# Cross attention on one core: another order of the three score banks within a step

## Chip, cores and metric

One NeuronCore of a Trainium2 chip runs the whole kernel. The metric is the device time of one execution in microseconds. All inputs and outputs are fp32.

## What is computed

The reference is one cross-attention layer with 32 heads of 32 columns, batch 2, 512 queries and 1024 keys per batch, hidden size 1024 (cut to what matters; `mu` and `var` are the mean and variance of a row):

```python
x = (hidden_states - mu) * rsqrt(var + 1e-5) * ln_gamma + ln_beta
Q = split_heads(x @ Wq.T);  K = split_heads(ctx);  V = split_heads(ctx)
scores = einsum('bhsd,bhtd->bhst', Q, K) * 32 ** -0.5
probs = softmax(where(mask, scores, -inf), axis=-1)
out = hidden_states + einsum('bhst,bhtd->bhsd', probs, V) @ Wout.T
```

## The kernel before

**Stages.** The kernel first normalises x and projects the queries (until about 141 us of the trace), then runs 16 attention steps (about 141 to 615 us), then multiplies the attention output by Wout and adds x (to the end). The change touches the attention steps alone.

**A step** is one batch and one group of four heads. Its 1024 keys are cut into eight tiles of 128; a tile with its four heads is a *slot*, `tt` = 0 to 7. So a step has 32 score blocks, numbered `at = 4 * tt + h`, 0 to 31. I call them score 0 to score 31, and their exponentials exp 0 to exp 31. For a score block:

- TensorE (L958, in `score`) multiplies a 99 x 128 block of keys with 99 x 512 of queries into one of three PSUM banks, `SX[at % 3]`.
- ScalarE (L624, in `exp`) reads that bank and writes the exponential into `PR`, a ring of four tiles in SBUF.
- TensorE (L974, in `values`) multiplies the four finished blocks of a tile with the values into the bank `PV`. This is called for the tile before the current one, so `values` of tile 7 runs within slot 0 of the next step.

**The wait that the change is about.** A score block may be written only after the exponential that last read its bank. Within a step, score `at` waits for exp `at - 3` (`pe.wait_ge(exp_done, PROBS * n + at - BANKS + 1)`, L953). For the first three scores of a step, L955 takes the last block of the step before that used the same bank. 32 blocks over three banks leave a remainder of two: score 30 uses bank 0 and score 31 uses bank 1, and the next step begins again with banks 0 and 1.

**What stands around it on TensorE.** The order is written out by hand in the table `STEP`. Per slot: scores 4tt and 4tt+1, the items `early`, `values` of the tile before, the items `with_01`, scores 4tt+2 and 4tt+3, the items `with_23`. The items are row maxima for the next steps (L934 on TensorE into one of two pairs of banks, `MX`, then a maximum on VectorE, L746), a transpose of keys (L874 in slot 0, copied by ScalarE at L550), a transpose of the maxima (L939), and the row sums of the step before (L964 in slot 1, 24 matrix multiplies with 32 columns of ones over the probabilities). All engines run their instructions in program order and wait on semaphores.

**The others.** GpSimd (L495) adds the probabilities of tiles 0 to 5 of a step into `acc`, five additions. ScalarE may overwrite a tile of `PR` only after GpSimd's addition that reads it. In slot 0, ScalarE also copies `PV` out (L628). SyncE issues the DMAs, among them the two bias rows (L350, L351) that score 0 of the next step waits for (`bias_in`).

**Where the steps stand in the program.** Step 0 is written out with a table of its own, `FIRST_STEP`. Steps 1 to 12 are three passes of a loop over four steps (`Fori`) on every engine. Steps 13, 14 and 15 are written out again. In step 15 the maxima are replaced by transposes of Wout (L944).

Of the kernel before, what the change touches and what calls it, by code (L numbers as in the profile page):

```python
# [27 lines left out]
ACT = mybir.ActivationFunctionType  # L28
# [4 lines left out]
P = 128  # L33
HPG = P // HD
# [7 lines left out]
RING = 4  # L42
MASK = 3 * HD
BIAS = MASK + 1
ROWS = BIAS + 2
SCALE = float(HD) ** -0.5
# [3 lines left out]
BIG = 1.75 * 2.0 ** 127  # L50
BANKS = 3
PROBS = TT * HPG
POOL_TILES = (0, 1, 2, 3, 4, 5)
DIRECT_TILES = (6, 7)
ADDS = len(POOL_TILES) - 1
DVE_T = 32
# [60 lines left out]
def is_first(n):  # L117

    return isinstance(n, int) and n == 0
# [57 lines left out]
def build(nc, x, ctx, mask, wq, wout, gamma, beta, out):  # L177
    def sb(name, shape, dt):
        return nc.alloc_sbuf_tensor(name, shape, dt)
# [11 lines left out]
    KS = [R[:, r * KSZ:(r + 1) * KSZ].rearrange("p (h t) -> p h t", h=HPG) for r in range(RING)]  # L191
    QS = [R[:, q_at[r]:q_at[r] + QSZ].rearrange("p (h s) -> p h s", h=HPG) for r in range(RING)]
# [22 lines left out]
    PR = sb("PR", [P, RING, HPG, S], F32)  # L215
# [32 lines left out]
    SX = [nc.alloc_psum_tensor(f"SX{i}", [P, S], F32) for i in range(BANKS)]  # L248
    PV = nc.alloc_psum_tensor("PV", [P, S], F32)
    QP = [PV, SX[2]]  # L250
# [19 lines left out]
    scores_ready, exp_done, tile_used, pool_used = sem("scores_ready"), sem("exp_done"), sem("tile_used"), sem("pool_used")  # L270
# [23 lines left out]
    with nc.Block() as block:  # L294
# [167 lines left out]
        def _(pool):  # L462
# [22 lines left out]
            def add_probs(n, k):  # L485

                first, tt = POOL_TILES[0], POOL_TILES[k + 1]
                if k == 0:
                    if not is_first(n):
                        pool.wait_ge(sums_done, n)  # L490
                else:
                    pool.wait_ge(pool_used, ADDS * n + ADDS + k)
                pool.wait_ge(exp_done, PROBS * n + HPG * (tt + 1))
                a = PR[:, first % RING, :, :] if k == 0 else acc[:, :, :]
# [25 lines left out]
        def _(act):  # L520
# [92 lines left out]
            def exp(n, tt, h):  # L613

                q = PROBS * n + HPG * tt + h
                if h == 0:

                    act.wait_ge(tile_used, TT * n + tt + 1)

                    old, m = (tt - RING, n) if tt >= RING else (tt + RING, n - 1)  # L620
                    if old in POOL_TILES:
                        act.wait_ge(pool_used, ADDS * m + ADDS + max(POOL_TILES.index(old), 1))
                act.wait_ge(scores_ready, q + 1)
                nc.scalar.activation(PR[:, tt % RING, h, :], SX[(HPG * tt + h) % BANKS][:, :], ACT.Exp, scale=SCALE).then_inc(exp_done, 1)  # L624

            def pv_copy(n):
                act.wait_ge(pv_done, n + 1)
# [16 lines left out]
            def step(n, items, at, first=False):  # L644
                for tt, (early, with_01, with_23) in enumerate(items):
                    exp(n, tt, 0)
                    exp(n, tt, 1)
                    if tt == 0 and not first:
                        pv_copy(n - 1)
                    at = high_and_bias(n, early + with_01, at)  # L650
                    exp(n, tt, 2)
                    exp(n, tt, 3)
                    at = high_and_bias(n, with_23, at)
                    if isinstance(n, int) and n == STEPS - 1 and tt == TT // 2:
                        first_attn_high()
# [206 lines left out]
        def _(pe):  # L862
# [84 lines left out]
            def score(n, u, tt, h):  # L947
                at = HPG * tt + h
                if at == 0:
                    pe.wait_ge(bias_in, 32 * (n + 1))  # L950

                if at >= BANKS:
                    pe.wait_ge(exp_done, PROBS * n + at - BANKS + 1)  # L953
                elif not is_first(n):
                    pe.wait_ge(exp_done, PROBS * n - PROBS + max(b for b in range(PROBS) if b % BANKS == at) + 1)  # L955
                elif SX[at] is QP[1]:
                    pe.wait_ge(q_copied, 2 + BATCH * GROUPS)
                nc.tensor.matmul(SX[at % BANKS][:, :], KS[u % RING][0:ROWS, h, tt * P:(tt + 1) * P], QS[u % RING][0:ROWS, h, :],  # L958
                                 start=True, stop=True).then_inc(scores_ready, 1)

            def sum_probs(bank, tile, start, stop):
# [6 lines left out]
            def values(n, u, tt):  # L968

                pe.wait_ge(exp_done, PROBS * n + HPG * (tt + 1))  # L970
                if tt == 0 and not is_first(n):
# [4 lines left out]
                if tt == TT - 1:  # L976
                    ins.then_inc(pv_done, 1)
                if tt in POOL_TILES:
                    ins.then_inc(tile_used, 1)
# [29 lines left out]
            at = 2 + len(WITH_GROUP[0])  # L1009
            pe.wait_ge(rows_in[0], FIRST_ROWS)  # L1010
            for g in range(1, GROUPS):
# [21 lines left out]
                at = end  # L1033
            pe.sem_inc(tile_used, RING)

            def step(n, u, items, at, loads, freed, first=False):
# [22 lines left out]
                for tt, (early, with_01, with_23) in enumerate(items):  # L1059
                    score(n, u, tt, 0)  # L1060
                    score(n, u, tt, 1)
                    for item in early:
                        mx_item(*item)
                    if tt >= 1:
                        values(n, u, tt - 1)
                    elif not first:
                        values(n - 1, u + RING - 1, TT - 1)
                    for item in with_01:
                        mx_item(*item)
                    score(n, u, tt, 2)  # L1070
                    score(n, u, tt, 3)
                    for item in with_23:
                        mx_item(*item)
# [3 lines left out]
            with pe.Fori(0, LOOPS) as j:  # L1077
                for u in range(1, RING + 1):
                    n = RING * j + u
# [3 lines left out]
            n = STEPS - 1  # L1083
# [49 lines left out]
```

## Time and profile before

| | |
|---|---|
| Median of 3 runs | 709.5 us (709.37 to 710.46) |
| The profiled execution | 710.47 us |
| Its span, first to last instruction | 708.6 us |
| TensorE busy, share of the span | 676.6 us, 95% |
| VectorE, ScalarE, GpSimd busy | 453.3, 339.4, 392.2 us |
| Mean granted TensorE clock | 0.998 |

The profile is of one execution. The 1.9 us between its time and its span lie before the first and after the last instruction. A busy TensorE is not a TensorE that issues at full rate: matrix multiplies overlap and their ends are modelled, so a late one shows as a longer one. The rows of its weight loads (PEld) carry the idle time and the releaser, and are read for waits.

### The profile page before, as it was taken

How to read it: one execution, taken by the hardware profiler on the slowest of the kernel's cores; microseconds unless marked ns; L12 is line 12 of the kernel's file. 1: busy time of each engine (PE TensorE's matmuls, PEld its weight loads, DVE VectorE, ACT ScalarE, POOL GpSimd, SP SyncE). 2: the span in 40 equal slices, each digit the busy share in tenths (PEclk: the TensorE clock that was granted, in tenths of full speed). 3: DMA queues.
4: the chain of work that ended last, by engine and by line, in shares of the span. 5: the costliest groups of instructions: out<-in, count | busy, mean ns of one | idle time of the engine just before them, and what ended most of it. 6: DMA issues, size and time to landing. Idle time of an engine off the chain costs nothing.

```text
span 708.6 us, 10761 instructions
## 1 busy us (share of the span) xinstructions
PE 676.6 (95%) x3537; PEld 395.6 (56%) x3537; DVE 453.3 (64%) x494; ACT 339.4 (48%) x614; POOL 392.2 (55%) x107
## 2 busy tenths in 40 slices
PE   2799999989999999999999999999999999999998
PEld 2577787844445454454544545445454454578886
DVE  6764343068878778687786877868778576633231
ACT  3641121256566665666656566565665666400000
POOL 1000000066679797697977979779797797900000
PEclk9999999999999999999999999999999999999999
DMA  9712000454624525245252452523515104033131
GB/s 337 196 39 71 31 30 1 93 123 108 149 59 108 128 64 138 56 110 122 67 138 65 100 125 65 138 65 100 134 32 134 61 7 144 31 118 114 65 118 59
DMA packets 40286, 68.10 MB, mean 96 GB/s; under 512 B 5668, under 2 KB 22694, under 8 KB 40238
## 3 DMA queue, kind: packets, MB, share of 16 engines
q1 hardware_dynamic: 39956, 67.25, 34.8%
q10 hardware_dynamic: 292, 0.40, 0.2%
q8 instruction: 17, 0.28, 0.2%
q14 instruction: 21, 0.17, 0.1%
HBM read 25.18 MB, written 4.19 MB: 41 GB/s over the span
## 4 chain that ended last, share of the span: by engine, by line
PE 89%; DVE 3%; ACT 3%; issue 2%; DMA 1%; SPq 1%; POOL 0%; ACTq 0%; DVEq 0%; POOLq 0%
PE MX L934 20%; PE PV L974 18%; PE SX L958 18%; PE MX L1092 12%; PE MX L964 5%; PE PV L897 5%; PE SX L897 5%; PE MX L874 2%; PE SX L889 1%; ACT PR L624 1%; PE MX L944 1%; DMA PR<-in_x 1%; ACT PR L534 1%; PE MX L868 1%; DVE R L705 1%
## 5 line engine op out<-in xcount | busy, mean ns | idle before, releaser
L746 DVE TENSOR_REDUCE mx<-MX 128x1 f32<-128x1024 f32 x256 | 301.8, 1216 | 87.3 <-PE MX L934 82.6
L624 ACT ACTIVATE PR<-SX 128x512 f32<-128x512 f32 x512 | 268.8, 600 | 161.2 <-PE SX L958 155.9
L495 POOL TENSOR_TENSOR acc<-acc,PR 128x2048 f32<-128x2048 f32 x64 | 293.7, 4589 | 8.7 <-POOL acc L495 5.4
L495 POOL TENSOR_TENSOR acc<-PR 128x2048 f32<-128x2048 f32 x16 | 73.5, 4594 | 219.1 <-ACT PR L624 219.1
L934 PE MATMUL MX<-R 97*128 97x512 f32 x512 | 174.5, 424 | 4.2 <-DMA R<-QT 1.5
L958 PE MATMUL SX<-R 99*128 99x512 f32 x512 | 174.0, 416 | 3.5 <-ACT PR L624 3.1
L934 PEld LDWEIGHTS MX<-R 97*128 97x128 f32 x512 | 84.5, 188 | 99.6 <-DVE mx L746 81.3
L974 PE MATMUL PV<-PR,C 128*32 128x512 f32 x1024 | 137.2, 608 | 0.1
L958 PEld LDWEIGHTS SX<-R 99*128 99x128 f32 x512 | 93.6, 189 | 66.5 <-ACT PR L624 35.5
L843 DVE TENSOR_TENSOR PR<-PR,MX 128x512 f32<-128x512 f32 x16 | 10.9, 686 | 53.3 <-PE MX L1092 51.7
L1092 PE MATMUL MX<-R 128*128 128x512 f32 x192 | 44.3, 390 | 0.0
L974 PEld LDWEIGHTS PV<-PR,C 128*32 128x32 f32 x1024 | 20.2, 108 | 41.2 <-ACT PR L624 36.4
L1092 PEld LDWEIGHTS MX<-R 128*128 128x128 f32 x192 | 36.0, 188 | 8.3 <-issue 0.8
L1092 PE MATMUL MX<-R,KTh 128*128 128x512 f32 x128 | 40.2, 390 | 0.0
L897 PE MATMUL PV<-R 128*128 128x512 f32 x120 | 32.3, 416 | 0.2 <-DVE R L705 0.2
L709 DVE TENSOR_TENSOR KTl<-MX,KTh 128x1024 fp32r<-128x1024 f32 x15 | 18.4, 1224 | 19.1 <-ACT KTh L550 19.1
L964 PE MATMUL MX<-PR,ones 128*32 128x512 f32 x240 | 28.5, 592 | 0.0
L1092 PEld LDWEIGHTS MX<-R,KTh 128*128 128x128 f32 x128 | 24.0, 188 | 5.8 <-issue 0.8
L483 POOL TENSOR_TENSOR QA<-QA,rsum 128x512 f32 (+1 forms) x16 | 20.6, 1289 | 11.4 <-DVE rsum L768 11.4
L572 ACT ACTIVATE QA<-SX 128x512 f32<-128x512 f32 x8 | 4.8, 599 | 44.3 <-PE SX L897 44.3
L897 PE MATMUL SX<-R,KTh 128*128 128x512 f32 x80 | 25.5, 389 | 0.0
L897 PEld LDWEIGHTS PV<-R 128*128 128x128 f32 x120 | 22.8, 199 | 4.8 <-DVE R L705 0.7
(84 smaller groups left out, 475.0 us busy)
## 6 DMA issues: line engine op xcount, KB each, us to landing
R<-KTh SPq DMA_DIRECT2D x60, 256.0 KB, 4.3
PR<-in_x SPq DMA_DIRECT2D x16, 512.0 KB, 4.1
C<-in_ctx SPq DMA_DIRECT2D x16, 512.0 KB, 3.4
R<-QT SPq DMA_DIRECT2D x62, 128.0 KB, 2.5
R<-KTl SPq DMA_DIRECT2D x60, 128.0 KB, 3.8
acc<-in_L_xattn_Wq SPq DMA_DIRECT2D x8, 512.0 KB, 3.7
C<-in_L_xattn_Wout SPq DMA_DIRECT2D x8, 512.0 KB, 3.4
R<-QT SPq DMA_DIRECT2D x62, 64.0 KB, 2.1
```

The source lines that it names most:

```text
L483: nc.gpsimd.tensor_tensor(at, at, rsum[:, :], ALU.mult).then_inc(attn_done, 1)
L495: nc.gpsimd.tensor_tensor(acc[:, :, :], a, PR[:, tt % RING, :, :], ALU.add).then_inc(pool_used, 1)
L624: nc.scalar.activation(PR[:, tt % RING, h, :], SX[(HPG * tt + h) % BANKS][:, :], ACT.Exp, scale=SCALE).then_inc(exp_done, 1)
L709: nc.vector.tensor_tensor(KTl[:, :], MX[par][:, :], KTh[:, :].bitcast(F32), ALU.subtract).then_inc(kt_lo, 1)
L746: nc.vector.tensor_reduce(mx[:, u % 2, i:i + 1], MX[par][:, :], mybir.AxisListType.X, ALU.max, negate=True).then_inc(mx_freed, 1)
L874: ins = nc.tensor.transpose(MX[par][:, t * P:(t + 1) * P], C[u % RING][:, t, :], ident[:, :])
L897: ins = nc.tensor.matmul(QP[b if bank is None else bank][:, :], w[W_IN[g]][:, k * P:(k + 1) * P], v[b][:, k, :], start=(k == 0 and o == 0) ...
L934: ins = nc.tensor.matmul(MX[par][:, cs], QS[u % RING][0:BIAS, h, st * P:(st + 1) * P], KS[u % RING][0:BIAS, h, cs], start=True, stop=True)
L958: nc.tensor.matmul(SX[at % BANKS][:, :], KS[u % RING][0:ROWS, h, tt * P:(tt + 1) * P], QS[u % RING][0:ROWS, h, :], start=True, stop=True). ...
L964: ins = nc.tensor.matmul(bank[h * HD:(h + 1) * HD, :], ones[:, :], tile(h), start=start, stop=stop, skip_group_check=True)
L974: ins = nc.tensor.matmul(PV[h * HD:(h + 1) * HD, :], C[u % RING][:, tt, h * HD:(h + 1) * HD], PR[:, tt % RING, h, :], start=(tt == 0), sto ...
L1092: ins = nc.tensor.matmul(MX[1 - q][:, cs], a[q][:, g, :], w[half][:, g, :], start=(g == 0 and o == 0), stop=(g == GROUPS - 1 and o == 2))
```

## The change

The bank of a score block is given by a new function `bank(b)`. Blocks 0 to 5 keep banks 0, 1, 2, 0, 1, 2. From block 6 on the order is turned by one: 6 uses bank 1, 7 bank 2, 8 bank 0, and so on, to 29 on bank 0, 30 on bank 1 and 31 on bank 2. The next step begins with bank 0 again. `before(b)` gives the block that used the bank of `b` last, as a negative number where it is in the step before: score 0 now waits for exp 29, score 1 for exp 30, score 2 for exp 31 of the step before. Score 6 now waits for exp 4 (before: exp 3), score 7 for exp 5 (before: exp 4), score 8 for exp 3 (before: exp 5). All others are as before.

```diff
+def bank(b):
+
+    return b % BANKS if b < HPG + 2 else (b + 1) % BANKS
+
+
+def before(b):
+
+    return max(c for c in range(-PROBS, b) if bank(c % PROBS) == bank(b))
...
-                nc.scalar.activation(PR[:, tt % RING, h, :], SX[(HPG * tt + h) % BANKS][:, :], ACT.Exp, scale=SCALE).then_inc(exp_done, 1)
+                nc.scalar.activation(PR[:, tt % RING, h, :], SX[bank(HPG * tt + h)][:, :], ACT.Exp, scale=SCALE).then_inc(exp_done, 1)
...
-                if at >= BANKS:
-                    pe.wait_ge(exp_done, PROBS * n + at - BANKS + 1)
-                elif not is_first(n):
-                    pe.wait_ge(exp_done, PROBS * n - PROBS + max(b for b in range(PROBS) if b % BANKS == at) + 1)
-                elif SX[at] is QP[1]:
+                if before(at) >= 0 or not is_first(n):
+                    pe.wait_ge(exp_done, PROBS * n + before(at) + 1)
+                elif SX[bank(at)] is QP[1]:
                     pe.wait_ge(q_copied, 2 + BATCH * GROUPS)
-                nc.tensor.matmul(SX[at % BANKS][:, :], KS[u % RING][0:ROWS, h, tt * P:(tt + 1) * P], QS[u % RING][0:ROWS, h, :],
+                nc.tensor.matmul(SX[bank(at)][:, :], KS[u % RING][0:ROWS, h, tt * P:(tt + 1) * P], QS[u % RING][0:ROWS, h, :],
                                  start=True, stop=True).then_inc(scores_ready, 1)
```

The order of work on TensorE stays; the banks, the values waited for and a few register instructions that compute these values move. Two places show it. First, TensorE where step 0 goes over into step 1: scores 30 and 31, the last maxima of the step, then scores 0 and 1 of the next and its `values`. Before:

```order
L958 MATMUL SX0<-R 128x512 [waits exp_done]
L958 MATMUL SX1<-R 128x512 [waits exp_done]
...
L1077 ISA
L955 ISA [waits bias_in]
L958 MATMUL SX0<-R 128x512 [waits exp_done]
L958 MATMUL SX1<-R 128x512 [waits exp_done]
L970 ISA
L974 MATMUL PV<-PR,C0 32x512 [waits exp_done]
```

And with the change:

```order
L968 MATMUL SX1<-R 128x512 [waits exp_done]
L968 MATMUL SX2<-R 128x512 [waits exp_done]
...
L1087 ISA
L965 ISA [waits bias_in]
L968 MATMUL SX0<-R 128x512 [waits exp_done]
L965 REGISTER_ALU
L968 MATMUL SX1<-R 128x512 [waits exp_done]
L980 ISA
L984 MATMUL PV<-PR,C0 32x512 [waits exp_done]
```

Bank 0 is now written three blocks before score 0, not two, and one register instruction stands between scores 0 and 1.

Second, TensorE in slot 1, after the row sums (the last of them reads `acc`): scores 6 and 7, one maximum, scores 8 and 9. Before:

```order
L964 MATMUL MX1<-acc,ones 32x512 x3
L958 MATMUL SX0<-R 128x512 [waits exp_done]
L953 REGISTER_ALU
L958 MATMUL SX1<-R 128x512 [waits exp_done]
L1042 REGISTER_ALU
L934 MATMUL MX0<-R 128x512 [waits mx_freed]
L934 MATMUL MX0<-R 128x512
L953 REGISTER_ALU
L958 MATMUL SX2<-R 128x512 [waits exp_done]
```

And with the change:

```order
L974 MATMUL MX1<-acc,ones 32x512 x3
L965 REGISTER_ALU
L968 MATMUL SX1<-R 128x512 [waits exp_done]
L965 REGISTER_ALU
L968 MATMUL SX2<-R 128x512 [waits exp_done]
L1052 REGISTER_ALU
L946 MATMUL MX0<-R 128x512 [waits mx_freed]
L946 MATMUL MX0<-R 128x512
L968 MATMUL SX0<-R 128x512 [waits exp_done]
```

Scores 6 and 7 now take the banks of scores 4 and 5, and a register instruction has moved from ahead of score 8 to ahead of score 6.

## Rows read from the trace of the kernel before

**Rows 1.** The page, busy time of each engine
```profile
PE 676.6 (95%) x3537; PEld 395.6 (56%) x3537; DVE 453.3 (64%) x494; ACT 339.4 (48%) x614; POOL 392.2 (55%) x107
```
**Rows 2.** Who waited for whom: us in total, times, longest us
```profile
PEld MX L934 <- DVE mx L746: 81.3, 121, 1.0
PEld PV L974 <- ACT PR L624: 36.4, 111, 0.4
PEld SX L958 <- ACT PR L624: 35.5, 123, 2.0
```
**Rows 3.** Busy time per engine from score 0 of step 6 to score 0 of step 7
```profile
320.22:349.54 29.32, 29.32 (x162) 14.18 (x161) 22.91 (x24) 18.52 (x36) 24.20 (x7) 1.00 0.40 99
```
**Rows 4.** Timeline, entry to step 6: start, duration, instruction, [idle before it <- releaser]
```profile
319.33 2.36 DVE L746 TENSOR_REDUCE mx<-MX 128x1 f32<-128x1024 f32 x2 [0.46 <-PE MX L934]
...
319.57 2.27 ACT L624 ACTIVATE PR<-SX 128x512 f32<-128x512 f32 x4 [1.08 <-PE SX L958]
319.57 4.59 POOL L495 TENSOR_TENSOR acc<-acc,PR 128x2048 f32<-128x2048 f32 x1 [0.16 <-POOL acc L495]
319.60 0.63 PE L934 MATMUL MX<-R 97*128 97x512 f32 x2
320.22 0.19 PEld L958 LDWEIGHTS SX<-R 99*128 99x128 f32 x1 [0.42 <-ACT PR L624]
...
320.70 0.19 PEld L958 LDWEIGHTS SX<-R 99*128 99x128 f32 x1 [0.30 <-ACT PR L624]
321.14 0.16 PEld L974 LDWEIGHTS PV<-PR,C 128*32 128x32 f32 x8 [0.25 <-issue]
...
322.13 0.30 PEld L934 LDWEIGHTS MX<-R 97*128 97x128 f32 x2 [0.84 <-DVE mx L746]
```
**Rows 5.** Timeline, the same pattern inside a step (step 5, slots 3 to 4)
```profile
306.25 2.07 ACT L624 ACTIVATE PR<-SX 128x512 f32<-128x512 f32 x4 [1.65 <-PE SX L958]
306.28 0.63 PE L934 MATMUL MX<-R 97*128 97x512 f32 x2
...
306.90 0.19 PEld L958 LDWEIGHTS SX<-R 99*128 99x128 f32 x1 [0.19 <-ACT PR L624]
...
307.38 0.16 PEld L974 LDWEIGHTS PV<-PR,C 128*32 128x32 f32 x8 [0.30 <-ACT PR L624]
```
**Rows 6.** Timeline, weight loads at the entries to step 2 and to step 14
```profile
202.59 0.19 PEld L958 LDWEIGHTS SX<-R 99*128 99x128 f32 x1 [0.30 <-ACT PR L624]
203.02 0.16 PEld L974 LDWEIGHTS PV<-PR,C 128*32 128x32 f32 x8 [0.25 <-issue]
...
555.76 0.19 PEld L958 LDWEIGHTS SX<-R 99*128 99x128 f32 x1 [0.24 <-ACT PR L624]
...
556.19 0.16 PEld L974 LDWEIGHTS PV<-PR,C 128*32 128x32 f32 x8 [0.25 <-issue]
```
**Rows 7.** Timeline, entry to step 1
```profile
172.92 0.42 PEld L958 LDWEIGHTS SX<-R 99*128 99x128 f32 x2
```
**Rows 8.** Timeline, entry to step 5, where the loop turns: exp 0, score 3
```profile
292.68 1.09 ACT L624 ACTIVATE PR<-SX 128x512 f32<-128x512 f32 x2 [2.19 <-issue]
...
293.33 0.19 PEld L958 LDWEIGHTS SX<-R 99*128 99x128 f32 x1 [0.83 <-ACT PR L624]
```
**Rows 9.** Timeline, entry to step 15: scores 0 and 1, values
```profile
584.24 0.52 PEld L958 LDWEIGHTS SX<-R 99*128 99x128 f32 x2
...
584.99 0.16 PEld L974 LDWEIGHTS PV<-PR,C 128*32 128x32 f32 x8 [0.24 <-issue]
```
**Rows 10.** Timeline, slot 1 of step 6: exps 4 and 5, scores 6 and 7
```profile
325.25 1.08 ACT L624 ACTIVATE PR<-SX 128x512 f32<-128x512 f32 x2
...
328.19 0.30 PEld L958 LDWEIGHTS SX<-R 99*128 99x128 f32 x2 [0.84 <-issue]
```
**Rows 11.** The last bias DMA before step 6, and such DMAs' us to landing
```profile
316.88 0.59 SPq L351 DMA_DIRECT2D R<-BTl  x1
...
R<-BTl SPq DMA_DIRECT2D x16, 8.0 KB, 1.8
```

## The prediction

> **What bounds the kernel now.** I read the page first. TensorE is busy 95% of the span, no other engine over 64% [rows 1], so what counts in the attention steps is what delays TensorE. The busy share hides this: over one step TensorE reads as busy for all 29.32 us, VectorE for 22.91, ScalarE for 18.52, GpSimd for 24.20 [rows 3], because a late matrix multiply is booked as a long one. The weight loads show the waits. Next I read who waited for whom: weight loads waited 35.5 us in total for exponentials ahead of scores, in 123 places, and 36.4 us ahead of values, in 111 [rows 2]. Most of this only mirrors the rate of the matrix multiplies. So the question has to be put place by place: when does a weight load start later than the instructions ahead of it on TensorE would let it?
>
> At the entry to a step it does. The last maximum of step 5 starts at 319.60 on TensorE. The load for score 0 comes at 320.22 after 0.42 us idle for an exponential, the one for score 1 at 320.70, after another 0.30, and the values of the last tile at 321.14 [rows 4]. ScalarE began exp 30 at 319.57 [rows 4]. Four exponentials in a row take 2.07 us where nothing holds them [rows 5], the last of them counted to its end at about 0.60, so they start (2.07 - 0.60) / 3 = 0.49 apart. Exp 30 then ends at 319.57 + 0.60 = 320.17 and exp 31 at 320.66. Score 0 started 0.05 after the end of exp 30 and score 1 about 0.05 after the end of exp 31: these are exactly the two waits that the remainder of two causes.
>
> The same stretch inside a step shows how it runs without them. There the maximum starts at 306.28, the second score at 306.90 and the values at 307.38, 1.10 us after the maximum [rows 5]. At the entry it takes 321.14 - 319.60 = 1.54 [rows 4]. The difference is 0.44 us.
>
> **What the change takes away.** Score 0 now waits for exp 29, which is over; score 1 for exp 30 (over at 320.17); and values, as before, for exp 31. So values can start at 320.66 + 0.05 = 320.71 and not at 321.14, a gain of 0.43. It can't be more, since values read what exp 31 writes. Both ways of working it agree, so I take 0.43 a place. Now the places, of the 15 entries:
>
> - *Entries to steps 2 to 4, 6 to 8 and 10 to 14, eleven in all.* They show the same pattern. From score 1 (just behind exp 31) to values it is 203.02 - 202.59 = 0.43 at the first and 556.19 - 555.76 = 0.43 at the last [rows 6]. 11 x 0.43 = 4.73 us.
> - *Entry to step 1.* Both loads run together without a wait [rows 7], since three maxima stand behind score 31 in that table. Zero.
> - *Entries to steps 5 and 9, where the loop turns.* ScalarE starts exp 0 only at 292.68 after 2.19 us that nothing explains but its own issue, and score 3, which needs exp 0's bank before and after, waits 0.83 for it [rows 8]. Values would come earlier, but the next score pair would not. Bounds: 0 and 0.43 each. I take 0, since that wait follows at once.
> - *Entry to step 15.* Scores 0 and 1 at 584.24 and values at 584.99 [rows 9]: 0.75, where the loads of a pair with no wait between them take 0.30 [rows 10]. Bounds 0 and 0.45. Half of it may be lost to ScalarE, which is the next to be waited for, so I take 0.2.
>
> Sum: 4.73 + 0.2 = 4.9 us.
>
> **What it adds, and what moves.**
>
> - *Scores 6 and 7 wait for exps 4 and 5.* These start at 325.25 and are over at 326.33; scores 6 and 7 are loaded from 328.19 on, behind the values and the 24 multiplies of the row sums [rows 10]. The cover is 328.19 - 326.33 = 1.86 us. Cost zero. Score 8 waits for an older exponential than before: nothing.
> - *A register instruction between scores 0 and 1* and one moved ahead of score 6. Scores 6 and 7 have one between them today and their two loads still take 0.30 us together [rows 10]. Score 1 has from 320.22 to 320.71 to be ready. Cost zero; from above, 0.1 at each of twelve places in the loop, 1.2 us.
> - *The bias rows.* Score 0 also waits for them. Issue at 316.88 and 1.8 us to landing [rows 11] give 318.7, while score 0 would now start about 0.4 earlier than 320.22, at 319.8. Still 1.1 us to spare.
> - *VectorE.* The first maximum after the values needs the `MX` half that the first of two reductions frees, 319.33 + 1.18 = 320.5 [rows 4]; it would start at 322.13 - 0.43 = 321.70. Free.
> - *GpSimd.* Its last addition ends at 319.57 + 4.59 = 324.16 [rows 4], and exp 4 may not start before, because it overwrites the tile. Exp 4 starts at 325.25 today [rows 10], at 324.82 with the change: 0.66 us are left. GpSimd's five additions begin with exp 7 of their step, so they move along and the rest does not shrink from step to step. This is the nearest thing that is late next.
>
> The profiled execution took 710.47 us, which gives 710.47 - 4.9 = 705.6. It is 1.0 above the median of 709.5, so for the median I forecast **704.6 us**.
>
> **Rivals.**
>
> 1. *The wait only moves.* Today the next bank is always the one free longest, except at the entry. The change puts the short distance in slot 1. If scores 6 and 7 stalled there for as long as 0 and 1 do today, the gain is given back, 15 x 0.43 against 11 x 0.43: about 709.5. Against it speaks the cover of 1.86 us. The Trainium skill ("Perfetto Trace Analysis", section on optimizing tensor performance, matmuls) says that independent groups should rotate through different PSUM banks so that the reading of one overlaps the next group; by this rule writing banks 1, 2, 1, 2 is worse than 1, 2, 0, 1, and this rival's time would be the result. The rows speak against it here, since the rule does not ask what stands between the two writes. 9%, together with the case that something I don't see binds every step.
> 2. *Half of it is swallowed downstream,* by GpSimd or by ScalarE, whose exp 4 has only 0.66 us left: 2.4 us gained, 707.1. For it: cover that thin at each step. Against: the distance is the same at each step. 8%.
> 3. *More.* Entries to 5 and 9 pay too, and step 15 in full: 13 x 0.43 + 0.45 = 6.0, so 703.5. 8%.
> 4. *Slower.* TensorE runs in order, so if exp 5 ended later than score 7 wants, row maxima and all behind it would wait. ScalarE has the key copy and GpSimd's tile ahead of exp 4. It decides from exp 5 ending 1.86 us later on; to lose what was gained too, 1.86 + 0.43 = 2.3 us. At 2.7 us it would cost 0.4 x 14 = 5.6 us more than it brings, 715.1. Even the turn of the loop on ScalarE, 2.19 us [rows 8], would not reach this point, and it comes twice. 3%.
>
> **How the numbers follow.** The forecast has 72%: 11 gains at 0.42 to 0.44, step 15 between 0 and 0.45, register instructions between 0 and 1.2 us. That is 4.6 - 1.2 = 3.4 to 5.2, so 704.3 to 706.1. The three runs of before spread by 1.1 us. With rival 3 at the lower end and the upper bound plus half of that spread at the upper, the range is 703.4 to 706.6; left out are rivals 1, 2 and 4, 20%. A measurement of this kernel can tell about 0.2%, 1.4 us, from no change. Faster by more: 72 + 8 + 8 = 88%. Within it: 9%. Slower: 3%.
>
> **What would show it.** In the trace after: at the entry to a step, scores 0 and 1 loaded at the pace of the row pair inside a step, with the wait ahead of score 0 gone and the one ahead of score 1 at 0.2 or less; values 1.10 us after the last maximum, not 1.54; four exponentials in 2.07 us there, not 2.27; a step of 28.9 us, not 29.32, in eleven places, and the steps 1, 5 and 9 begun as late after their maxima as before; no exponential named as the releaser of scores 6 and 7. Wrong would be my account if values moved and the step did not shorten (rival 2), or if a wait for ScalarE appeared at score 6 (rivals 1 and 4).

## The result and the profile after

The changed kernel takes 705.12 us (median of 6 runs, 703.63 to 707.15) against 709.55 for the kernel before: ratio 0.9937, interval 0.992 to 0.9955. That is 4.4 us faster; forecast were 704.6 us and 4.9 us gained. The profiled execution took 705.0 us with a span of 703.2, forecast 705.6. One execution of the kernel before, among the 52 taken beside the experiments below, took 830.18 us at a granted clock of 0.759 and is left out here.

I read the time first by stages, since two single executions differ in places that the change does not touch. Each row runs from score 0 of a step or to it: start of the trace to step 0, step 1 to step 15, step 15 to the end. The columns are the stretch, its length, busy time (and count) of TensorE, weight loads, VectorE, ScalarE and GpSimd, granted clock, DMA share, GB/s. The kernel before:

```profile
0.00:140.86 140.86, 118.32 (x562) 97.41 (x563) 64.60 (x103) 43.52 (x55) 2.89 (x10) 1.00 0.32 99
172.92:584.24 411.32, 410.21 (x2256) 198.03 (x2255) 316.61 (x318) 257.73 (x489) 333.79 (x83) 1.00 0.38 94
584.24:708.60 124.36, 118.95 (x587) 85.72 (x585) 48.19 (x52) 19.57 (x36) 32.58 (x10) 0.99 0.27 93
```

The changed kernel, and in its last row one step, from score 0 of step 6 to score 0 of step 7:

```profile
0.00:140.12 140.12, 116.85 (x562) 96.30 (x563) 64.49 (x103) 43.27 (x55) 2.89 (x10) 0.96 0.33 99
172.38:578.87 406.49, 404.79 (x2255) 198.04 (x2254) 316.49 (x318) 256.80 (x489) 333.72 (x83) 1.00 0.38 95
578.87:703.20 124.33, 118.86 (x587) 85.66 (x585) 48.18 (x52) 19.58 (x36) 32.62 (x10) 0.99 0.27 93
...
318.08:346.96 28.88, 28.88 (x162) 14.19 (x161) 22.90 (x24) 18.41 (x36) 24.20 (x7) 1.00 0.41 100
```

The steps took 411.32 us and take 406.49: 4.83 us gained there. The last stage is the same to 0.03. The first stage differs by 0.7, in code that the change leaves alone; it goes with the clock, as the last section shows. Step 0, between the first two rows, takes 32.06 us and 32.26. One step takes 28.88 us where it took 29.32 [rows 3], with the same busy time on VectorE and GpSimd.

The timeline at the entry to step 6, in the changed kernel, answers to [rows 4] (lines of `exp`, `score` and `values` are now L636, L968 and L984):

```profile
317.81 2.07 ACT L636 ACTIVATE PR<-SX 128x512 f32<-128x512 f32 x4 [1.08 <-PE SX L968]
317.84 0.63 PE L946 MATMUL MX<-R 97*128 97x512 f32 x2
318.08 0.19 PEld L968 LDWEIGHTS SX<-R 99*128 99x128 f32 x1
...
318.46 0.19 PEld L968 LDWEIGHTS SX<-R 99*128 99x128 f32 x1 [0.19 <-ACT PR L636]
318.94 0.16 PEld L984 LDWEIGHTS PV<-PR,C 128*32 128x32 f32 x8 [0.30 <-ACT PR L636]
```

The wait ahead of score 0 is gone, the one ahead of score 1 is 0.19, and the values start 318.94 - 317.84 = 1.10 us after the last maximum, not 1.54. Four exponentials take 2.07 us, not 2.27. The entry reads like the inside of a step [rows 5].

Where the loop turns, at the entry to step 5, the values come early too, but exp 0 and score 3 do not:

```profile
288.01 0.19 PEld L968 LDWEIGHTS SX<-R 99*128 99x128 f32 x1
...
288.88 0.16 PEld L984 LDWEIGHTS PV<-PR,C 128*32 128x32 f32 x8 [0.30 <-ACT PR L636]
...
290.93 1.08 ACT L636 ACTIVATE PR<-SX 128x512 f32<-128x512 f32 x2 [2.10 <-PE SX L968]
291.57 0.19 PEld L968 LDWEIGHTS SX<-R 99*128 99x128 f32 x1 [1.17 <-ACT PR L636]
```

The row of exp 0 names score 0 as its releaser, but score 0 was loaded at 288.01, 2.9 us before. The wait of score 3 has grown from 0.83 [rows 8] to 1.17, and the step takes 30.07 us where it took 30.16.

In slot 1 of step 6, exps 4 and 5 and scores 6 and 7:

```profile
323.06 1.08 ACT L636 ACTIVATE PR<-SX 128x512 f32<-128x512 f32 x2
...
325.99 0.30 PEld L968 LDWEIGHTS SX<-R 99*128 99x128 f32 x2 [0.84 <-issue]
```

Exp 5 ends at 324.14, scores 6 and 7 load from 325.99 on: 1.85 us of cover, as forecast (1.86), and no exponential is named. In all 16 steps the cover is at least 1.72 us.

### The profile page after: what moved, and what is told of

Its sections match the earlier page's. It is cut to its first block, busy times and chain, and to the rows that moved or that the text cites. A ratio compares the mean times of both kernels' runs of the same rounds, so it can differ in the third digit from the quotient of the medians.

```text
span 703.2 us, 10761 instructions
## 1 busy us (share of the span) xinstructions
PE 669.5 (95%) x3537; PEld 394.5 (56%) x3537; DVE 453.2 (64%) x494; ACT 338.2 (48%) x614; POOL 392.2 (56%) x107
## 4 chain that ended last, share of the span: by engine, by line
PE 89%; DVE 3%; ACT 3%; DMA 2%; issue 2%; SPq 1%; POOL 0%; ACTq 0%; DVEq 0%; POOLq 0%
PE MX L946 20%; PE PV L984 18%; PE SX L968 17%; PE MX L1102 12%; PE MX L974 5%; PE SX L909 5%; PE PV L909 5%; PE MX L886 2%; DMA PR<-in_x 1%; ACT PR L636 1%; PE SX L901 1%; PE MX L956 1%; ACT PR L546 1%; PE MX L880 1%; DVE R L717 1%
## 5 line engine op out<-in xcount | busy, mean ns | idle before, releaser
L636 ACT ACTIVATE PR<-SX 128x512 f32<-128x512 f32 x512 | 268.0, 601 | 159.7 <-PE SX L968 157.0
L968 PE MATMUL SX<-R 99*128 99x512 f32 x512 | 170.0, 412 | 4.2 <-ACT PR L636 3.9
L984 PE MATMUL PV<-PR,C 128*32 128x512 f32 x1024 | 137.3, 608 | 0.1
L968 PEld LDWEIGHTS SX<-R 99*128 99x128 f32 x512 | 93.5, 189 | 60.8 <-ACT PR L636 31.0
L984 PEld LDWEIGHTS PV<-PR,C 128*32 128x32 f32 x1024 | 20.2, 108 | 42.0 <-ACT PR L636 40.6
```

Source lines behind the costliest of these rows:

```text
L636: nc.scalar.activation(PR[:, tt % RING, h, :], SX[bank(HPG * tt + h)][:, :], ACT.Exp, scale=SCALE).then_inc(exp_done, 1)
L968: nc.tensor.matmul(SX[bank(at)][:, :], KS[u % RING][0:ROWS, h, tt * P:(tt + 1) * P], QS[u % RING][0:ROWS, h, :], start=True, stop=True).th ...
L984: ins = nc.tensor.matmul(PV[h * HD:(h + 1) * HD, :], C[u % RING][:, tt, h * HD:(h + 1) * HD], PR[:, tt % RING, h, :], start=(tt == 0), sto ...
```

## Experiments

All times are medians; ratios are against the kernel before, run on the same chip between them. The first four experiments ran on one chip and the last four on another. The kernel before had a median of 710.4 us (707.05 to 714.32 over 29 runs) beside the first four and also 710.4 (707.82 to 711.34 over 22) beside the last four.

**The change once more.** No edit.

> The changed kernel once more, with more rounds, beside the kernel before on the same chip. Theory (two waits at each step entry are gone): about 4.5 to 5 us faster than before, near 705. The first runs spread over 3.5 us against 1.1 for before: if the change causes the spread, it shows again here; if it is chance, both kernels spread alike.

705.36 us, ratio 0.9941 (0.9919 to 0.9963): 5.0 us faster. The spread of 3.5 us in the first runs is not the change's own: this time the changed kernel spread over 2.4 us (6 runs) and the kernel before over 7.3 (29 runs).

**Score 0 waits as before.** This edit and those of the next four experiments are made to the changed kernel.

```diff
-                    pe.wait_ge(exp_done, PROBS * n + before(at) + 1)
+                    held = before(at) + (at == 0)
+                    pe.wait_ge(exp_done, PROBS * n + held + 1)
```

> Banks as in the changed kernel, but score 0 waits for exp 30 again, as it did before the change. Theory: score 0 at the entry has time until exp 31 ends, so this wait is free: within 0.5 us of the changed kernel, about 705. Rival (the wait of score 0, 0.42 us long in the rows, costs its length): 11 times 0.42, back to 709.5.

707.73 us, ratio 0.9961 (0.9945 to 0.9978). Neither side was right: about half of the gain is lost. Weight loads at the entry to step 6:

```profile
319.57 0.30 PEld L969 LDWEIGHTS SX<-R 99*128 99x128 f32 x2 [0.42 <-ACT PR L636]
320.24 0.16 PEld L985 LDWEIGHTS PV<-PR,C 128*32 128x32 f32 x8 [0.36 <-ACT PR L636]
```

After its wait the pair needs 320.24 - 319.57 = 0.67 us until the values can load. Exp 30, which released it, and exp 31 are only 0.49 apart. So TensorE itself is late by 0.67 - 0.49 = 0.18 a time, and the step takes 29.06 us, not 28.88. Over the 13 entries to steps 2 to 14, less the two where the loop turns, that is 2.0 us; the medians differ by 2.4.

**Score 1 waits as before.**

```diff
-                    pe.wait_ge(exp_done, PROBS * n + before(at) + 1)
+                    held = before(at) + (at == 1)
+                    pe.wait_ge(exp_done, PROBS * n + held + 1)
```

> Banks as in the changed kernel, but score 1 waits for exp 31 again, as it did before the change, and score 0 does not wait. Theory: the multiply of score 1 then stands between exp 31 and the values, so all of the gain goes: 11 times 0.43 plus 0.1, about 709.5. Rival (each of the two waits costs its share, 0.42 and 0.30): some 3 us back, 708.

710.78 us, ratio 1.0000 (0.9983 to 1.0017). The whole gain is gone by this one wait:

```profile
320.43 0.19 PEld L969 LDWEIGHTS SX<-R 99*128 99x128 f32 x1
321.30 0.19 PEld L969 LDWEIGHTS SX<-R 99*128 99x128 f32 x1 [0.68 <-ACT PR L636]
321.73 0.16 PEld L985 LDWEIGHTS PV<-PR,C 128*32 128x32 f32 x8 [0.25 <-ACT PR L636]
```

Score 0 runs at once, and the values still come 321.73 - 321.30 = 0.43 behind score 1, which waits for exp 31. The step takes 29.33 us.

**Both waits as before, on the new banks.**

```diff
-                    pe.wait_ge(exp_done, PROBS * n + before(at) + 1)
+                    held = before(at) + (at <= 1)
+                    pe.wait_ge(exp_done, PROBS * n + held + 1)
```

> Banks as in the changed kernel, both waits of before put back. Theory: the banks themselves cost nothing, the time is that of the kernel before, 709.5. If score 6 and 7 on the banks of 4 and 5 cost anything, it is slower than before by that.

710.05 us, ratio 1.0000 (0.9982 to 1.0018). So the order of the banks by itself costs and brings nothing that shows: the interval is 0.18% to either side, and in the profiles steps 1 to 15 take 411.44 us, against 411.32 in the kernel before. It works by the two waits alone, and these do not add: 0.18 an entry for the first alone, 0.44 for the second, 0.44 for both.

```profile
320.39 0.19 PEld L969 LDWEIGHTS SX<-R 99*128 99x128 f32 x1 [0.42 <-ACT PR L636]
320.87 0.19 PEld L969 LDWEIGHTS SX<-R 99*128 99x128 f32 x1 [0.30 <-ACT PR L636]
321.30 0.16 PEld L985 LDWEIGHTS PV<-PR,C 128*32 128x32 f32 x8 [0.25 <-issue]
```

**The turn at block 8.**

```diff
-    return b % BANKS if b < HPG + 2 else (b + 1) % BANKS
+    return b % BANKS if b < 2 * HPG else (b + 1) % BANKS
```

> The order of banks is turned at block 8 in place of block 6, so scores 8 and 9 reuse the banks of 6 and 7 with one row maximum between, the same surroundings as at the step entry of the kernel before. Theory (cover decides, not distance alone): the values of slot 2 start 0.43 us later in all 16 steps, 6.9 us, against 4.9 gained at the entries: about 712, slower than before. Rival (only the entries are special, for their register and bias instructions): 705.

712.65 us, ratio 1.0032 (1.0016 to 1.0049): slower than before, as expected. The short distance now stands where only a row maximum lies between, and the rows of the old entry reappear at scores 8 and 9 of step 6:

```profile
330.97 0.19 PEld L968 LDWEIGHTS SX<-R 99*128 99x128 f32 x1 [0.42 <-ACT PR L636]
331.46 0.19 PEld L968 LDWEIGHTS SX<-R 99*128 99x128 f32 x1 [0.30 <-ACT PR L636]
331.89 0.16 PEld L984 LDWEIGHTS PV<-PR,C 128*32 128x32 f32 x8 [0.25 <-issue]
```

The steps inside the loop take 29.33 us as before the change. What makes it slower than the kernel before are the steps whose entry gained little or nothing and which now pay in slot 2. From the values of one step to those of the next, steps 5 and 9 take 0.35 and 0.45 more, steps 14 and 15 together 0.4. Step 0 takes 2.1 more in this profile; some 0.4 of it is the new wait, and for the rest the granted clock was at 0.66 for 5 us, which I estimate at 5 x 0.34 = 1.7:

```profile
147.00:152.00 5.00, 5.00 (x17) 2.00 (x17) 3.00 (x4) 1.80 (x4) 4.31 (x1) 0.66 0.44 119
```

So it stood at the lower level, 1.2 GHz, for about two thirds of these 5 us. The edit is not needed for it: the profile with both waits as before shows the same from 146 to 151 us (0.66). But it may come more often with the edit. Seven of the ten runs of this version have a mean granted clock of 0.987, 0.988 or 0.995 (the profiled one 0.995), against three of the 22 of the kernel before beside them. Of its other three, the run at 0.993 took 709.28 us, where the kernel before took 708.33 at 0.993, and the run at 0.997 took 711.85, where the kernel before took 710.36 to 711.34. So at the same clock, from one run each, the edit costs about 1 us, and whether it also brings on the rest is open.

**The turn at block 10.**

```diff
-    return b % BANKS if b < HPG + 2 else (b + 1) % BANKS
+    return b % BANKS if b < 2 * HPG + 2 else (b + 1) % BANKS
```

> The order of banks is turned at block 10: scores 10 and 11 reuse the banks of 8 and 9, with one values group and one row maximum between, and no row sums. Theory: exps 8 and 9 follow exp 7 at 0.49 us each, while the values and the maximum take 1.0 + 0.3 us from the end of exp 7 on, so some 0.3 us of cover are left: the same as the changed kernel, 705. Rival (the row sums were needed as cover): slower by up to 16 x 0.4.

704.47 us, ratio 0.9932 (0.9906 to 0.9959), a step of 28.88 us. At scores 10 and 11, 329.11 us, the timeline shows a pair without a wait, right behind a values group (L984) and a maximum:

```profile
327.77 0.16 PEld L984 LDWEIGHTS PV<-PR,C 128*32 128x32 f32 x8 [0.30 <-ACT PR L636]
328.77 0.30 PEld L946 LDWEIGHTS MX<-R 97*128 97x128 f32 x2 [0.84 <-DVE mx L758]
329.11 0.42 PEld L968 LDWEIGHTS SX<-R 99*128 99x128 f32 x2
```

So the row sums are not needed as cover; one values group is enough.

**Steps 1 to 12 written out, changed kernel.** `LOOPS = 0`, and each engine's loop over it becomes a Python loop that is not entered (cut to one of the five engines):

```diff
-    LOOPS = STEPS // RING - 1
+    LOOPS = 0
...
-            with pe.Fori(0, LOOPS) as j:
+            for j in range(LOOPS):
```

> The changed kernel with steps 1 to 12 written out in place of the loop. Theory: ScalarE's 2.2 us without work at the entries to steps 5 and 9 come from the turn of the loop; without it these two steps take 28.9 us, not about 30.0, and the change's gain comes there too: 705 - 2.2 = 703. Rival (fetching twice as much code costs as much): 705 or more, with idle time named issue spread over the steps.

701.37 us, ratio 0.9878 (0.9855 to 0.9901), the fastest version of this study. It gained more than expected: 4.0 us on the 705.36 of the changed kernel, which was measured on the other chip, where the kernel before had the same median.

```profile
287.31:316.12 28.81, 28.81 (x163) 14.12 (x161) 22.91 (x24) 18.68 (x36) 24.25 (x7) 1.00 0.41 102
```

Step 5 takes 28.81 us, not 30.07, and step 9 likewise 28.81, not 29.87 (the two together 2.3 us). The other ten steps of the loop are each about 0.08 shorter as well, 0.8 us, which I had not expected and did not look into. Together this is 3.1 of the 4.0 us; what is left is within the spread of the runs (four here).

**Steps 1 to 12 written out, kernel before.** The same edit on the kernel before.

> The kernel before with steps 1 to 12 written out. Theory: the two turns cost about 0.85 and 0.55 us: 709.5 - 1.4 = 708. The difference to the changed kernel written out is then 13 x 0.43 + 0.2, some 5.8 us. Rival (the entries to steps 5 and 9 would not pay): the difference stays 4.9.

708.36 us, ratio 0.997 (0.9956 to 0.9984).

```profile
290.21:319.45 29.24, 29.16 (x161) 14.12 (x162) 22.91 (x24) 18.75 (x36) 24.22 (x7) 1.00 0.40 101
```

Step 5 takes 29.24, and every step from 2 to 14 about 0.44 more than in the changed kernel written out, 13 x 0.44 = 5.7 us; the medians differ by 7.0. In the two profiles the steps from 1 to 15 took 408.9 and 403.2 us, 5.7 apart, and nearly all of the rest lies ahead of step 1. So the entries to steps 5 and 9 do pay once the turn of the loop is gone: that turn, and nothing in the banks, had hidden the gain. The edit takes the loop from all five engines; that ScalarE's turn is the one that counts is read from the rows, where score 3 waits for exp 0.

## Why the prediction was right

**The time.** 705.1 measured, 704.6 forecast, inside the range of 703.4 to 706.6. The gain at the medians was 4.4 us in the first runs and 5.0 in the second, so 4.9 is met no closer than that. Term by term, taking the start of the values of each step in the profiles of before and after:

| Term | Forecast | Measured |
|---|---|---|
| Entries to steps 2, 3, 6 to 8, 10 to 14 | 10 x 0.43 | 10 x 0.44 |
| Entry to step 4 | 0.43 | 0.29 |
| Entries to steps 5 and 9, net of what score 3 gives back | 0 | 0.07 and 0.04 |
| Entry to step 15 | 0.2 | 0.14 |
| Sum | 4.9 | 4.9 |

The second profile of the changed kernel gives 4.7: the entry to step 4 pays 0.42 there, and step 9 comes out at -0.16 and not 0.04. The profiled execution was 0.6 us faster than forecast (705.0 for 705.6), and about as much (0.7) came from the first stage, which no term of the forecast covers.

**The mechanism.** The step that carried the forecast, that score 1 stands between exp 31 and the values, is shown: putting this one wait back takes the whole gain. That the register instruction between scores 0 and 1 is free is shown by the rows of the changed kernel, where the values start 0.05 after exp 31 ends at the entries to steps 2, 3 and 5 to 14.

**Where it was inexact.** Among the signs it named, one did not come: steps 5 and 9 were to begin as late after their maxima as before. They began early (the values of step 5 at 288.88, 1.10 us after the maximum), and what was gained was lost again at score 3. The part on the places had said so, the list of signs had not. At step 15 the upper bound of 0.45 set the 0.75 us from score 0 to the values against the 0.30 that two loads take. But such a pair needs 579.53 - 578.87 = 0.66 us to the values in the changed kernel too, so little more than the 0.14 that came was to be had; the 0.2 was near by a halving, not by a reading. And 11 x 0.44 + 0.45 is 5.3, not 5.2, which changes no bound of the range.

The prediction priced both waits together and did not say what each is worth. Going by its remark that score 1 has until exp 31 ends, the expectation for the single wait of score 0 called it free; it costs 0.18 an entry, because after a stall the pair takes 0.67 us to the values and the exponentials are 0.49 apart. This had no part in the sum, since the change removes both waits.

**The bias rows.** The text gave score 0 1.1 us to spare, from a landing after 1.8 us. That is the median. At the entry to step 4 of the changed kernel's profile, the DMA was issued at 256.00 and landed 3.2 us later, and score 0 had to wait for it:

```profile
DMA to landing us min/median/max: 1.8/1.8/3.2
...
256.00 0.59 SPq L363 DMA_DIRECT2D R<-BTl  x1
...
259.32 0.30 PEld L968 LDWEIGHTS SX<-R 99*128 99x128 f32 x2 [0.40 <-ACT PR L636]
```

The profile puts the wait down to ScalarE, but exp 29 had ended at 257.62; the landing at 259.2 fits. In the profiles with score 1 held and with the turn at block 8 too, score 0 of step 4 is loaded 0.12 us after such a landing. It is the 0.14 missing at step 4 in the table. In the second profile of the same kernel this DMA was in time and the entry paid in full. The kernel before hid such a landing behind its own wait. A wait that is removed thus uncovers the tail of another, here only now and then.

**The rivals.** *The wait only moves* is excluded for block 6 by the rows of slot 1, and shown to be real for block 8. The Trainium skill's advice to rotate through different PSUM banks ("Perfetto Trace Analysis", optimizing tensor performance, matmuls) asks for other banks and nothing about how far apart two uses of one must be. So by itself it would have the kernel before and all three turns alike, since each has one pair of blocks that reuses banks two blocks later. The kernel before takes 710.4 us, blocks 6 and 10 give 705.4 and 704.5, block 8 712.7. The measurement decides: what counts is the work between the two writes. *Half is swallowed*: GpSimd's last addition ends at 317.80 + 4.60 = 322.40 in the changed kernel and exp 4 starts at 323.06, the 0.66 us forecast:

```profile
317.80 4.60 POOL L507 TENSOR_TENSOR acc<-acc,PR 128x2048 f32<-128x2048 f32 x1 [0.16 <-POOL acc L507]
```

Inside the loop it is 0.64 or more at every step, in step 13 0.58. In steps 14 and 15 it is 0.08, but it was 0.10 and 0.08 before the change too. *More*: not in the loop, but it appears at steps 5 and 9 with the steps written out; step 15 did not pay in full there either. *Slower* by late exps 4 and 5 did not show, with 1.72 us or more of cover in every step.

## What to carry to other kernels

When a number of blocks is not a multiple of the number of banks, the rotation wraps at a short distance somewhere; it need not be where the period of the program wraps. Put it where the engine has most other work between the two writes, and check that work against the time in which the reader drains the bank (here 1.3 us of it are enough, and one row maximum is not). Of several waits in a row on one engine, price the last one first: it can cost everything, and the others only what they push past it.

## What the runs showed of the hardware that I had not expected

**At a turn of the loop ScalarE stood idle for 1.9 to 2.3 us** between exp 31 and exp 0, twice in the kernel, in each of the eight profiles with a loop. On TensorE nothing shows: score 0 of step 5 is loaded without a wait in the rows above. The turn made two steps 0.6 to 1.2 us longer and hid the change's gain in them. Writing the steps out removed it. At the medians that edit gained 4.0 us for the changed kernel and 2.0 for the kernel before, not all of it from the turns. Why ScalarE stands idle for so long is not settled by these runs.

**The column of the granted clock can read 1.00 where TensorE runs at its lower level.** From 20 to 30 us, in code that the change does not touch, the view gives 1.00 for the kernel before and 0.63 for the changed kernel:

```profile
20.00:30.00 10.00, 6.42 (x23) 5.40 (x24) 6.61 (x16) 5.50 (x8) 0.00 (x0) 1.00 0.76 169
20.00:30.00 10.00, 6.04 (x28) 5.17 (x29) 6.72 (x17) 5.95 (x9) 0.00 (x0) 0.63 0.76 172
```

Read from this alone, the clock dropped in the second execution only. The same four transposes tell otherwise, before the change (L889) and after it (L901):

```profile
25.78 1.05 PE L889 MATMUL SX<-ident,PR 128*128 128x128 f32 x4
27.91 1.05 PE L889 MATMUL SX<-ident,PR 128*128 128x128 f32 x4
29.79 0.60 PE L889 MATMUL SX<-ident,PR 128*128 128x128 f32 x4
...
26.15 1.05 PE L901 MATMUL SX<-ident,PR 128*128 128x128 f32 x4
27.88 0.60 PE L901 MATMUL SX<-ident,PR 128*128 128x128 f32 x4
```

They take 1.05 us in both kernels at first and 0.60 later. The changed kernel's column says 0.50, 1.2 GHz, from 24 to 26 us. So both stood at that level here, and the changed kernel came to 2.4 GHz about 2 us sooner. In the four profiles in which the short durations come only at 29.7 to 29.8 us the first stage takes 140.8 to 140.9 us, whatever the kernel; in the six others it takes 139.2 to 140.4. The 0.7 us of the first stage go with this, and the mean clocks 0.998 and 0.990 of the two profiles do not compare.

**Short stretches at the lower level go with the spread between runs of one kernel.** Of the runs of the kernel before beside the experiments, the four with a mean granted clock of 1.000 took 707.05 to 707.82 us, and the sixteen with 0.997 took 710.31 to 711.34. What sets them off was not tested.
